# Norm factors finished for two steps at a time, and both rotary products of a step in one VectorE instruction

## The reference

```
q, k, v = split(shift_tokens(x) @ Wqkv[i])       # 16 heads of 64
q = q / max(norm(q), 1e-12) * q_scale            # l2norm, the same for k
q = q * cos * scale + rotate_half(q) * sin * scale
k = k * cos / scale + rotate_half(k) * sin / scale
out = local_attention(q, k, v)                   # windows of 32, each sees itself and the one before
x = out @ Wo[i] + x
x = ffn(shift_tokens(x)) + x                     # layer norm, W1, a * gelu(gate), W2
```

## Time and profile before

| what | value |
|---|---|
| time, median of 3 runs | 2242.39 us (2242.22 to 2244.29) |
| the profiled execution | 2249.67 us, span 2247.8 us |
| granted TensorE clock, mean | 0.970 |
| busy share of the span | PE 90%, DVE 72%, ACT 66%, POOL 55% |

### The profile page before, as it was taken

The page is one execution under the profiler, slowest core; times in us unless marked ns, Lnnn a source line. Parts: engine busy times, 40 slices in busy tenths (PEclk is TensorE's granted clock), DMA queues, the critical chain, the costliest instruction groups (busy, mean ns, idle before and its releaser), DMA issues. The chain is left out here.

```text
span 2247.8 us, 85596 instructions
## 1 busy us (share of the span) xinstructions
PE 2015.2 (90%) x32996; PEld 1382.4 (62%) x32996; DVE 1627.7 (72%) x3071; ACT 1476.9 (66%) x4549; POOL 1236.7 (55%) x1377
## 2 busy tenths in 40 slices
PE   7797988998899998899988999998999889999987
PEld 3232335875775866766757758667667577586662
DVE  1598997985875966867857759668678587596673
ACT  4522225976775966867767759668677677596772
POOL 1465865664753654754646536548546465365450
PEclk9888789999999999999999999999999999999998
DMA  1311112111121211211111211112211111121010
GB/s 57 133 66 66 65 38 78 40 40 33 42 73 30 49 38 31 66 54 37 39 33 37 78 28 50 35 36 58 62 35 41 34 37 40 28 50 30 23 29 19
DMA packets 148105, 104.49 MB, mean 46 GB/s; under 512 B 15778, under 2 KB 140256, under 8 KB 146176
## 3 DMA queue, kind: packets, MB, share of 16 engines
q1 hardware_dynamic: 147712, 99.07, 15.8%
HBM read 48.31 MB, written 1.18 MB: 22 GB/s over the span
## 5 line engine op out<-in xcount | busy, mean ns | idle before, releaser
L1372 POOL TENSOR_TENSOR QK<-PC,PS 128x256 f32<-128x256 f32 x384 | 278.5, 725 | 612.9 <-DVE PS L1283 612.9
L1121 ACT ACTIVATE PR<-ps,MN 128x64 f32<-128x64 f32 x1536 | 353.7, 312 | 378.0 <-DVE MN L1243 377.8
L1377 POOL TENSOR_TENSOR QK<-QK,RN 128x512 f32<-128x512 f32 x384 | 400.4, 1043 | 159.5 <-ACT RN L1111 132.0
L995 PE MATMUL ps<-W,XS 128*128 128x256 f32 x1536 | 401.0, 384 | 4.1 <-PEq L64 4.1
L995 PEld LDWEIGHTS ps<-W,XS 128*128 128x128 f32 x1536 | 264.7, 193 | 26.8 <-issue 4.9
L1373 POOL TENSOR_TENSOR QK<-PC,PS 128x256 f32<-128x256 f32 x384 | 278.9, 726 | 0.0
L981 PE MATMUL ps<-ident,QK 128*128 128x128 f32 x1536 | 252.7, 287 | 26.0 <-POOL QK L1377 24.1
L1267 DVE TENSOR_REDUCE SS<-SQ 128x8 f32<-128x512 f32 x384 | 259.4, 676 | 4.5 <-ACT SQ L1154 4.4
L1281 DVE TENSOR_TENSOR PC<-ps,TC 128x512 f32<-128x512 f32 x384 | 261.4, 681 | 0.3 <-issue 0.3
L1283 DVE TENSOR_TENSOR PS<-ps,TS 128x512 f32<-128x512 f32 x384 | 260.0, 677 | 0.0
L1154 ACT ACTIVATE SQ<-ps 128x512 f32<-128x512 f32 x384 | 241.4, 629 | 20.4 <-PE ps L995 11.1
(11 more groups left out here) (138 smaller groups left out, 3457.0 us busy)
## 6 DMA issues: line engine op xcount, KB each, us to landing
V<-V SPq DMA_DIRECT2D x384, 97.5 KB, 2.2
scr<-B_rows SPq DMA_DIRECT2D x32, 512.0 KB, 3.7
V<-V SPq DMA_DIRECT2D x288, 32.5 KB, 1.9
W<-in_Wqkv SPq DMA_DIRECT2D x40, 192.0 KB, 2.8
TC<-in_tcos SPq DMA_DIRECT2D x6, 1024.0 KB, 5.3
TS<-in_tsin SPq DMA_DIRECT2D x6, 1024.0 KB, 7.6
WO<-in_Wo SPq DMA_DIRECT2D x6, 512.0 KB, 5.3
W<-in_W SPq DMA_DIRECT2D x6, 341.0 KB, 3.3
```

Of the source, the lines that this page charges most:

```text
L995: mm = nc.tensor.matmul(ps[:, par, k * 2 * P:(k + 1) * 2 * P], cols[k], W[:, i, 0:2, :].rearrange("p t m -> p (t m)"), start=True, stop=True)
L1121: e = nc.scalar.activation(PR[:, m % 2, h, slot * DH:(slot + 1) * DH], ps[:, 3 + h, slot * DH:(slot + 1) * DH], ACT.Exp, scale=-1.0, bias= ...
L1372: nc.gpsimd.tensor_tensor(QK[:, par, :, 0:hd], PC[:, par, :, 0:hd], PS[:, par, :, hd:DH], ALU.add)
L1377: nc.gpsimd.tensor_tensor(QK[:, par, :, :], QK[:, par, :, :], bcast_last(RN[:, par, :], DH), ALU.mult).then_inc(qk, 1)
```

## The change

1. `norms` takes the step's own squares (lag 0 where it was 1) and stands behind `tables` in VectorE's loop. The sum goes into half of a tile for two steps, and only after the second is the maximum taken, for 16 columns at once and with an immediate number where it was the tile LEAST.
2. On ScalarE `root` and `logs` become `norm_pair`, which at each even n takes Ln and then Exp for both steps n - 2 and n - 1 at the loop's head.
3. `tables` is one instruction over a joined table TCS: the step's 512 columns of PSUM are read twice and multiplied with cosine and sine, 1024 columns in all.
4. `rotate` takes lag 2 where it was 1.
5. On ScalarE `copy_v` stands ahead of `copy_p`.
6. TensorE's waits are sorted anew, so that each instruction of a plain step has at most one. Some go away as implied by others. The one on `v_cp` moves from `values(n)` to `scores(n)`; those on `pr` and `oT` move forward by a group.

```diff
             def scores(n):
...
-                wait(pe, pr, m)
-                wait(pe, oT, m - 3)
+                if n >= NSTEPS:
+                    wait(pe, pr, m)
+                    wait(pe, oT, m - 3)
                 for h in range(2):
+                    if h == 0:
+                        wait(pe, qkT, min(n - 3, NSTEPS))
+                    if h == 1 and n >= 7:
+                        pe.wait_ge(v_sh[(n - 7) % 4], 32 * ((n - 7) // 4 + 1))
                     nc.tensor.matmul(ps[:, 3 + h, 0:P], identb[:], MASKB[:, int(s == 0), h, :], start=True, stop=True)
-                pe.wait_ge(qkT, m + 1)
+                if n == 5:
+                    pe.wait_ge(qkT, m + 1)
+                wait(pe, v_cp, min(n, NSTEPS))
                 for slot in range(2):
...
             def values(n):
                 pe.wait_ge(pT, m + 1)
-                pe.wait_ge(v_sh[m % 4], 32 * (m // 4 + 1))
-                wait(pe, on, m)
-                wait(pe, v_cp, min(n, NSTEPS))
+                if n >= NSTEPS + 5:
+                    pe.wait_ge(v_sh[m % 4], 32 * (m // 4 + 1))
+                    wait(pe, on, m)
...
             def project(n):
-                wait(pe, v_cp, n)
-                wait(pe, on, n - 6)
+                if n < 5:
+                    wait(pe, v_cp, n)
                 for k in range(2):
+                    if k == 0:
+                        wait(pe, on, n - 6)
+                    if k == 1:
+                        wait(pe, pr, n - 4)
...
             def p_transposed(n):
-                pe.wait_ge(pr, m + 1)
-                wait(pe, pT, m)
-                wait(pe, on, m)
+                if n >= NSTEPS:
+                    pe.wait_ge(pr, m + 1)
+                    wait(pe, on, m)
+                if n < 7 or n >= NSTEPS + 5:
+                    wait(pe, pT, m)
                 for h in range(2):
+                    if h == 0 and n < NSTEPS:
+                        wait(pe, oT, n - 7)
...
+            def norm_pair(n):
+                p = n // 2 - 1
+                if n % 2 or not 0 <= p < NSTEPS // 2:
+                    return
+                act.wait_ge(ssm, p + 1)
+                nc.scalar.activation(SS[:, p % 2, :], SS[:, p % 2, :], ACT.Ln, scale=LN_SCALE).then_inc(lns, 1)
+                act.wait_ge(lns, p + 1)
+                wait(act, qk, 2 * p - 2)
+                nc.scalar.activation(RN[:, p % 2, :], SS[:, p % 2, :], ACT.Exp, scale=-0.5, bias=lnb[:]).then_inc(rn, 1)
...
-                root(n)
+                norm_pair(n)
                 exponents(n)
                 copy_out(n)
                 if u == U_FFN and t >= 0:
-                    logs(n)
                     load_set(nc, act, GELU)
                 copy_qk(n)
                 squares(n)
+                copy_v(n)
                 copy_p(n)
-                copy_v(n)
                 if u == U_FFN and t >= 0:
                     gates(t, n)
                     load_set(nc, act, EXP_LN)
-                else:
-                    logs(n)
...
             def norms(n):
+                p, k = n // 2, n % 2
+                dve.wait_ge(sq, n + 1)
+                wait(dve, rn, p - 1)
+                nc.vector.tensor_reduce(SS[:, p % 2, 8 * k:8 * k + 8], SQ[:, n % 2, :, :], AX.X, ALU.add).then_inc(ss, 1)
+                if k == 1:
+                    dve.wait_ge(ss, n + 1)
+                    nc.vector.tensor_scalar(SS[:, p % 2, :], SS[:, p % 2, :], 1e-24, None, ALU.max).then_inc(ssm, 1)
...
             def tables(n):
-                nc.vector.tensor_tensor(PC[:, par, :, :].rearrange("p (k a) d -> p k (a d)", k=2), src,
-                                        TC[l % 2][:, 2 * s:2 * s + 2, :], ALU.mult)
-                nc.vector.tensor_tensor(PS[:, par, :, :].rearrange("p (k a) d -> p k (a d)", k=2), src,
-                                        TS[l % 2][:, 2 * s:2 * s + 2, :], ALU.mult).then_inc(prods, 1)
+                both = TCS[l % 2][:, :, 2 * s:2 * s + 2, :].rearrange("p t k c -> p t (k c)")
+                nc.vector.tensor_tensor(PCS[:, par, :, :, :].rearrange("p t a d -> p t (a d)"),
+                                        ps[:, par, :].unsqueeze(1).to_broadcast([P, 2, CH]), both, ALU.mult).then_inc(prods, 1)
...
                 least(n)
                 normalise(n)
+                tables(n)
                 norms(n)
-                tables(n)
...
             def rotate(n):
-                m = n - 1
+                m = n - 2
...
-                pool.wait_ge(rn, m + 1)
+                pool.wait_ge(rn, m // 2 + 1)
```

More of the change, by code:

```diff
@@ L71, in mamba_block @@
         XT, XRES, XS, MOD, ident, ones, epsc = (keep[k] for k in ("XT", "XRES", "XS", "MOD", "ident", "ones", "epsc"))
-        W, QKS, QK4, TC, TS, MASKB, identb = (keep[k] for k in ("W", "QKS", "QK4", "TC", "TS", "MASKB", "identb"))
+        W, QKS, QK4, TCS, MASKB, identb = (keep[k] for k in ("W", "QKS", "QK4", "TCS", "MASKB", "identb"))
         ps = keep["ps"]
@@ L178, in _ @@
             sp.wait_ge(b_out[1], 16)
-            sp.dma_start(TC[0][:], d["tcos"]).then_inc(ld_tab, 16)
-            sp.dma_start(TS[0][:], d["tsin"]).then_inc(ld_tab, 16)
+            sp.dma_start(TCS[:, 0], d["tcos"]).then_inc(ld_tab, 16)
+            sp.dma_start(TCS[:, 1], d["tsin"]).then_inc(ld_tab, 16)
             for t in range(3):
@@ L788, in transformer_block @@
         SQ = sb("SQ", [P, 2, 8, DH])
-        PC = sb("PC", [P, 2, 8, DH])
-        PS = sb("PS", [P, 2, 8, DH])
+        PCS = sb("PCS", [P, 2, 2, 8, DH])
+        PC, PS = PCS[:, :, 0], PCS[:, :, 1]
         QK = sb("QK", [P, 2, 8, DH])
-        SS = sb("SS", [P, 2, 8])
-        RN = sb("RN", [P, 2, 8])
+        SS = sb("SS", [P, 2, 16])
+        RN = sb("RN", [P, 2, 16])
         MN = sb("MN", [P, 2, 4])
@@ L815, in transformer_block @@
         stored = [sem("stored%d" % c) for c in range(NCH)]
-        s_vz, s_ones, s_v0, s_lnb, s_least = (
-            sem(k) for k in ("s_vz", "s_ones", "s_v0", "s_lnb", "s_least"))
+        s_vz, s_ones, s_v0, s_lnb = (
+            sem(k) for k in ("s_vz", "s_ones", "s_v0", "s_lnb"))
         qkv_dram = d["Wqkv"].rearrange("l p (t i m) -> l p i t m", t=3, i=PAIRS)
@@ L843, in load_tables @@
             def load_tables(l):
-                sp.dma_start(TC[l % 2][:], d["tcos"]).then_inc(w_tab[l % 2], 16)
-                sp.dma_start(TS[l % 2][:], d["tsin"]).then_inc(w_tab[l % 2], 16)
+                sp.dma_start(TCS[l % 2][:, 0], d["tcos"]).then_inc(w_tab[l % 2], 16)
+                sp.dma_start(TCS[l % 2][:, 1], d["tsin"]).then_inc(w_tab[l % 2], 16)
             def load_w1(l):
@@ L925, in out_transposed @@
                     return
-                wait(pe, pr, min(n - 5, NSTEPS))
-                wait(pe, oT, m)
-                pe.wait_ge(on, m + 1)
+                if n >= NSTEPS:
+                    wait(pe, pr, min(n - 5, NSTEPS))
+                    wait(pe, oT, m)
+                    wait(pe, on, m + 1)
                 for k in range(2):
@@ L976, in qk_transposed @@
                 pe.wait_ge(qk, m + 1)
-                wait(pe, qkT, m)
+                if n < 5:
+                    wait(pe, qkT, m)
                 for x in range(2):
@@ L1103, in _ @@
             act.wait_ge(s_lnb, 1)
-            def root(n):
-                m = n - 2
-                if not 0 <= m < NSTEPS:
+            def norm_pair(n):
+                p = n // 2 - 1
+                if n % 2 or not 0 <= p < NSTEPS // 2:
                     return
-                act.wait_ge(lns, m + 1)
-                wait(act, qk, m - 1)
-                nc.scalar.activation(RN[:, m % 2, :], SS[:, m % 2, :], ACT.Exp, scale=-0.5, bias=lnb[:]).then_inc(rn, 1)
+                act.wait_ge(ssm, p + 1)
[3 more added lines that the diff above has]
+                nc.scalar.activation(RN[:, p % 2, :], SS[:, p % 2, :], ACT.Exp, scale=-0.5, bias=lnb[:]).then_inc(rn, 1)
             def exponents(n):
@@ L1234, in _ @@
         def _(dve):
-            dve.wait_ge(s_least, 1)
             def least(n):
@@ L1359, in scale_tables @@
                 pool.wait_ge(w_tab[l % 2], 32 * ((l + 1) // 2))
-                for tab in (TC, TS):
-                    piece = tab[l % 2][:, 2 * j:2 * j + 2, :]
+                for tab in range(2):
+                    piece = TCS[l % 2][:, tab, 2 * j:2 * j + 2, :]
                     nc.gpsimd.tensor_tensor(piece, piece, QK4[:].rearrange("p x h d -> p (x h d)").unsqueeze(1)
@@ L1421, in adaln_kernel @@
             "QK4": sb("QK4", [P, 2, 2, DH]),
-            "TC": [sb("TC0", [P, L // P, 2 * P])],
-            "TS": [sb("TS0", [P, L // P, 2 * P])],
+            "TCS": sb("TCS0", [P, 2, L // P, 2 * P]),
             "MASKB": sb("MASKB", [P, 2, 2, P], BF16),
```

18 lines of the change are left out of this document (5 added, 13 removed).

## The result

| | time (median) | span of the profiled execution |
|---|---|---|
| before | 2243.34 us (4 runs) | 2247.8 us |
| after | 2283.38 us (4 runs, 2276.9 to 2284.4) | 2280.3 us |

The ratio is 1.0173, 95% interval 1.0152 to 1.0193: slower by 40 us where +18 was forecast, and 1.4 us above the top of the range. The two spans differ by 32.5 us only, since the profiled execution of before was 6 us above its median and that of after was not.

What follows compares the result with a forecast made beforehand. A ring of dependences, no full engine, was taken to bound the kernel; the change would close one through V. Plain steps +28, rescaling -5, feed-forward parts -5: +18, 2260 us, range 2237 to 2282.

Steps and rivals of the forecast that it cites:

- the first mechanism: In plain steps, scores waiting for V close a ring of one step, 3.62 us (3.58 to 3.64).
- ring 2: Named after measuring: two-step loop MN, ON, joined product, R1, R2, maximum, Ln, Exp, PR, SQ, V, scores; 7.25 us.
- ring 1: One-step loop scores, MN, PR, QKT, SQ, V, next scores: forecast 3.62 us, read as 3.54 after the change.
- Rival 1: Plain steps: the ring through V does not bind, pace 3.30 to 3.40, 2187 to 2208 us; chance 0.14.
- rival 2: Same time: V's copy 0.38, no hold of the maximum, full gains elsewhere, 2240 us; chance 0.12.
- Rival 3: Maximum held up to 4.4 in odd steps makes RN late, 0.10 to 0.15 a step: 2277 to 2288 us; chance 0.12.
- the paragraph on GpSimd: Later `rotate` moves past `scale_tables`, saving 5 us (0 to 8) over five rescalings and costing nothing in plain steps.
- The semaphore term: From V's end to the matmul waiting for it: 0.11 us to the weight load plus 0.04.
- The late RN: Even plain steps: PR delayed 0 to 0.3 us in two steps by RN; taken as 0.02 a step.
- The hold: VectorE's maximum is held until GpSimd's running instruction is through: 0.166 us free, 0.437 in the median before.
- u = 15: Feed-forward step where the table load waits for Ln: at most 1.04 us saved, 0.7 taken; -7.7 us forecast.
- u = 7: Feed-forward step where the step's own squares precede the centring: about 0.3 us on the variance chain; +3.3 us forecast.

Runs made afterwards that it cites:

- run 7: The changed kernel without VectorE's maximum, the sum going to Ln with a constant bias: 2255.96 us, ratio 1.0056.
- run 9: The changed kernel without VectorE's maximum and with `rotate` at lag 1, the wait on V still at the scores: 2234.89 us, ratio 0.9956.
- run 2: The changed kernel with `rotate` back at lag 1, nothing else undone: 2256.91 us, ratio 1.0049.
- run 10: The changed kernel without VectorE's maximum and with the wait on V back at the values, `rotate` still at lag 2: 2215.13 us, ratio 0.9865.
- run 8: The changed kernel without VectorE's maximum, with the wait on V back at the values and `rotate` at lag 1: 2191.07 us, ratio 0.9762.
- run 6: The kernel before with the wait on `v_cp` moved to `scores` and `copy_v` ahead of `copy_p`, nothing else: 2281.38 us, ratio 1.0172.
- run 1: The changed kernel with the wait on V back at the value matmuls: 2280.23 us, ratio 1.0146.
- run 3: The changed kernel with the wait on V back at the values and `rotate` at lag 1: 2250.65 us, ratio 1.0029.
- run 11: The kernel before with its 384 maxima left out, a bias of Ln in their place: 2217.09 us, ratio 0.9874.
- Run 4: The changed kernel with TensorE's whole program and the order of `copy_p` and `copy_v` as before: 2272.94 us, ratio 1.0123.

## Why the prediction was right or wrong

**The direction was right, and the first mechanism exists.** The wait on V closes a ring, scores stand for V, PR still waits for MN, and runs 7 and 9 show the ring alone at 3.53 and 3.54 us. But at that length it costs next to nothing against before, whose plain steps took 3.53 in the mean: 2 us of the 21 at most. The other 19 are ring 2's, and what ring 1 does is to hide the 41 to 44 us that the rest could gain once the maximum is gone. Rival 1 (the ring does not bind) and rival 2 (the low ends) are out. Rival 3 (RN late) holds the measured time in its 2277 to 2288, but its sum is not what happened: it wanted plain steps of 3.72 to 3.77 us, and they took 3.63. Its sign, PR released by RN in the even steps 0.2 us late, is there in kind, at 0.18.

**The step that failed** is the paragraph on GpSimd: "`rotate` moves past `scale_tables`", and nothing else. With lag 2 it moves past every instruction that GpSimd has behind `rotate(n)`, and at u = 8 and 12 that is `affine`, which waits for a chain through TensorE, VectorE and ScalarE. At u = 12 the rotation that `qk_transposed` needs at n = 14 now stands behind that wait. Cost in the spans 16.6 + 5.9 = 22.5 us; the line as a whole costs 26.5 us in the medians by run 2, and 24.1 by runs 10 and 8. Without it after would stand at 2256.9 us, inside the range. At u = 8 the same wait costs next to nothing (+1.0 us in 11 steps). The prediction gave "GpSimd reaching TensorE through the later `rotate`" 0.04 and no price. The row to ask for was the wait of `affine` (L1387) in the trace of before: 39.8 us in only 2 of 24 instructions. In the other 22 GpSimd reached it after its input was there, held up by the rotation in front. So it was in before at u = 12, where the input was ready at 1467.04 + 0.63 = 1467.67:

```profile
POOL CEN L1387 <- ACT DEV L1192: 39.8, 2, 26.6
```

```profile
1467.04 0.63 ACT L1192 ACTIVATE DEV<-DEV 128x512 f32<-128x512 f32 x1
...
1468.00 1.04 POOL L1377 TENSOR_TENSOR QK<-QK,RN 128x512 f32<-128x512 f32 x1 [2.18 <-ACT RN L1111]
1469.00 1.27 POOL L1387 TENSOR_TENSOR CEN<-CEN,DEV 128x512 f32<-128x512 f32 x1
```

In after GpSimd comes early and stands, 24 times, 5.07 to 5.13 us in each of the 22 of the woven-in parts, and the next rotation stands behind it. In run 2, with lag 1, it also stands 24 times, but 1.63 to 1.68 us in these 22, and the rotation that TensorE needs is already done. So it is not the standing that costs, but what stands behind it.

**Two terms of the ring were mis-sized, in opposite directions.** The semaphore term was taken from a wait with others in front of it and carried to a place where the change leaves only one: 0.15 in the sum, 0.06 measured, 0.14 in run 6. The late RN was taken as 0.02 a step "near the low end"; it is 0.18 in two steps, 0.09 a step. R2 ended at 4.23 after the odd scores, in the middle of the 4.1 to 4.4 read off, not at the earliest. 3.54 + 0.09 = 3.63, where the prediction had 3.62 + 0.02 = 3.64: nearly the right pace out of two errors, which is luck. It mattered in run 1, where I had taken ring 2 for a small addition and it was a second bound of the same length.

The hold itself was read rightly from the earlier trace rows. The new maximum takes 174 ns at least and 304 in the median. In 158 of the 192 it took more than 200 ns, and each of these ended 0.03 us behind a GpSimd instruction that was running when it began; in the other 34 no instruction of GpSimd that ran at its start was still running at its end:

```profile
L1275 DVE TENSOR_SCALAR SS<-SS x192: 174/304/769, 368.3 to 2203.8; 128x16 f32<-128x16 f32 x192
```

The Trainium skill (DVE: opcode table, instruction layouts, handler registers and perf-mode slots, 7. Perf-mode slots) says that an instruction with one source can enter a 2-port mode at fp32 as well. By the rule weighed in the prediction such an instruction contends with GpSimd; the 304 ns agree with that, though no run here shows the mode itself, and the branch of the prediction without a hold was wrong.

**Right in size** were u = 15 (-9.1 for -7.7) and u = 7 (+2.5 for +3.3), and the joined product with 1.215 us for 1.20. The rescaling came out right in size too (-4.4 for -5), but for a wrong reason, so that is luck. The prediction took the gain from the later `rotate`. In each of the four pairs of kernels that differ in the lag alone, the 40 steps take longer with lag 2: 163.3 us against 159.2 (after and run 2), 165.6 against 160.4 (runs 1 and 3), 161.4 against 159.3 (runs 7 and 9), 161.9 against 159.0 (runs 10 and 8). So lag 2 costs 2 to 5 us there. The gain against the 167.7 of before is of other parts of the change; leaving the maximum out of before gives 5.0 of it (run 11, 162.7 us), and which part gives it in after stays open. The plain steps came out at +21 for +28, in part because the mean over all 216 of them was 3.53 before, not the 3.51 of the stretch read.

**What stays open.** Run 4 shows that the norms for two steps, VectorE's order, the joined product and lag 2 lose 30 us together, 20 of them at u = 13 and 14; which of the first three sets its pace of 3.61 was not taken apart beyond the maximum. Nor was a way tried to floor the sum on another engine, or to take the maximum where GpSimd is idle.

## What to carry to other kernels

Before a stage is given a later lag in an in-order queue, list everything that it moves behind, and look for the one whose own wait is long or has only just not been one: moving a stage later is free only if the queue it moves in has slack at every n. When a wait is put in front of work that used to run ahead, sum the terms from start to start around the loop, take the semaphore term from a wait of the same form, and then look for a second ring that is nearly as long, since undoing one alone shows little (3 us in run 1, 41 with the other open). A tiny VectorE instruction that is held by GpSimd is worth removing outright: leaving it out gave 22 to 65 us in the five kernels where it was tried, where 192 or 384 of them are no more than some 170 ns each when free.

## What the runs showed of the hardware

- A VectorE instruction of 16 fp32 columns with a single SBUF input takes 174 ns free; beside GpSimd's addition it ended 0.03 us behind that one (1419.15 and 1419.12 in after), 304 ns long in the median of after and 578 in run 1. A row sum of 512 fp32 columns from SBUF on the same engine was not held: 685 to 687 ns in all 384 of after, also where GpSimd's additions ran beside it (1418.14 in the timeline above).
- From the end of a copy on ScalarE to the start of the small matmul that waits for it: 0.06 us with one wait on the instruction (after, median of 384 steps 0.053), 0.14 with others ahead of it in the queue (run 6, median 0.144).
- A stretch of 4.00 us in which TensorE was busy 2.26 us, with an idle time of 1.51 us in it, was followed by a granted clock of 0.57 over the next 3.9 us, and by 0.99 after that. At u = 14 this made a step of 3.3 us one of 4.5 to 4.9 in 5 of 11 parts; in the other 6 the same step at u = 13 was followed by a clock of 1.00.
